# The values' products of layer 1 go two slots later in an order of instructions written by hand

## The chip, the cores and the metric

One core of a Trainium2 chip. The time is that of the whole kernel on the device, in microseconds (us), from one launch. TensorE is PE in the rows (PEld its weight loads), VectorE is DVE, ScalarE is ACT, GpSimd is POOL and SyncE, which issues most DMAs, is SP.

## The reference

Two transformer layers with a layer norm behind each half; batch 8, 512 tokens, width 256, all in float32.

```python
x = _layernorm(x + _L0_attn_ref(x, ...))   # 16 heads of 64, causal, latent of 64
x = _layernorm(x + _L0_ffn_ref(x, ...))    # 16 experts, the 2 best, and a shared one
x = _layernorm(x + _L1_attn_ref(x, ...))   # below
x = _layernorm(x + _L1_ffn_ref(x, ...))    # relu squared, 5 spiking steps
```

The change is in layer 1's attention. It has 16 heads of 16 columns per batch:

```python
q_c = jnp.einsum('bhtl,dl->bhtd', jnp.einsum('bhtd,ld->bhtl', xh, W_DQ), W_UQ)
q_c_norm = _rms_norm(q_c, q_norm_w)
q_r = jnp.einsum('bhtd,rd->bhtr', q_c_norm, W_QR)
kv = jnp.einsum('bhtl,dl->bhtd', jnp.einsum('bhtd,ld->bhtl', xh, W_DKV), W_UKV)
k_c, v_c = (kv[..., :HD], kv[..., HD:])
k_c_norm, k_r = _rms_norm(k_c, k_norm_w), jnp.einsum('bhtd,rd->bhtr', xh, W_KR)
scores = jnp.einsum('bhqd,bhkd->bhqk', q, k) * scale      # q = [q_c_norm, q_r], k = [k_c_norm, k_r]
ctx = jnp.einsum('bhqk,bhkd->bhqd', softmax(scores + causal), v_c)
out = jnp.einsum('bhtd,od->bhto', ctx, W_O)
```

The kernel multiplies the small matrices into four 128 x 128 ones beforehand (`w`: SQ for queries, SK for keys, SV for values with the output matrix in it, SG for the rotation part of the keys).

## The kernel before, in words

The kernel runs in blocks: layer 0's attention, its experts, and then one block for `layer1`. In that block every engine walks through the same list of slots, `SLOTS_ALL`, numbered from -52 to beyond 128, and issues in each slot what stands there. Nothing is scheduled by a tool: the order on each engine is the order of the code, and semaphores tie the engines together. Slots have no fixed length; a slot lasts as long as its work and its waits.

Slot n from 0 to 127 computes the scores of head n (`scores`, L1663, on TensorE, four tiles in the three banks `ps_score`) and VectorE takes the masked maximum of each tile (`mask_max`, L2037). Four heads make a quad. After a quad, TensorE turns its maxima (`turn_max`, L1673), ScalarE copies them (`keep_max`, L1874), and SyncE moves them by a DMA (`shifts`, L1474) into a row of the queries' buffer, so that the next product subtracts them. Seven slots behind (`BACK`), TensorE computes the same head's scores again, transposed and with the maximum taken off, in three groups (`exponents`, L1685): the first two behind the scores, the third at the very end of the slot, in two banks `ps_st` in turn. ScalarE takes the exponential of each group (`exps`, L1884), and GpSimd cuts off the triangle above the diagonal (`cut`, L1573). A quad's products with the values are in `attend` (L1701), in two slots per quad (remainder 0 and 1 of n by 4); `turn_back` (L1710) and VectorE's `outputs` (L2047 to L2054) finish them. `attend` waits until the `outputs` of the quad before are computed (L2049), since both use bank y.

What prepares queries, keys and values is the *front*. There is one per 8 heads, 16 in all. Each front f runs through steps, and `front_at(n, step)` tells which front has that step in slot n:

```python
def front_at(n, step):
    f, left = divmod(n + LEAD - step, HH)      # LEAD 23, HH 8
    return f if left == 0 and 0 <= f < NFRONT else None
```

So step s of front f stands in slot 8f + s - 23, and every step has a fixed remainder of the slot number by 8: step 12 has 5, steps 13 and 14 have 6 and 7, step 15 has 0. A turn of eight slots thus holds parts of three or four fronts. The steps are: -1 `turn` (L1607: x turned, into bank a), 0 `features` (ScalarE's copy of it, L1828), 1 and 2 `project` (L1619: queries, keys, bank b), 2 and 3 copies and squares (L1836, L1842), 3 and 4 `means` on VectorE (L2012), 5 to 8 GpSimd's root and `normed` (L1510 to L1530), 9 `turn_queries` (L1630, bank a), 10 the queries' high and low words (L1861, L1976), 11 `turn_keys` (L1640, bank b), 12 `weigh` on ScalarE (L1867) and on TensorE `values` (L1650, four products of 128 x 128 columns into bank a) and `rotation` (L1645, bank b), 13 `rotary` on VectorE (L2019) and `keep_values` on ScalarE (L1848: bank a into the values' buffer V), 14 the keys' high and low words (L1858, L1974). SyncE's `fill` (L1462, L1469, nine DMAs for a quad) then spreads the words into the buffers QS and KS.

Bank a is used in turn by `turn`, `turn_queries` and `values`. `turn` of front f waits for `keep_values` of front f - 2 (semaphore `vc`), and it stands in slot 8f - 24; `values` waits until the low words of the queries are out of bank a (`lo`). `attend` waits for `vc` too, 20 slots or more later. `keep_values` stands near the head of its slot on ScalarE, ahead of the slot's `exps`.

In every second turn (remainder by 16) there is more work: gathers of the experts' outputs on GpSimd, their mixing on VectorE (L1999), roots, and the norms' writes on ScalarE (L1890, L1896). Scores run from slot 0 on. Before it, fronts 0 and 1 run with TensorE mostly idle.

Of the kernel before, what the change touches and what calls it, by code (L numbers as in the profile page):

```python
# [1339 lines left out]
def layer1(nc, X, folded, slot, weight, Y, C, A):  # L1340

    with ExitStack() as ctx:
# [69 lines left out]
        def front_at(n, step):  # L1412

            f, left = divmod(n + LEAD - step, HH)
            return f if left == 0 and 0 <= f < NFRONT else None

        def turned(n):

            return (n - 5) // QUAD if 5 <= n < NHEADS + 5 and n % QUAD == 1 else None
# [31 lines left out]
        with nc.Block() as blk:  # L1451
# [147 lines left out]
            def _(pe):  # L1599
# [43 lines left out]
                def rotation(f):  # L1643
                    pe.wait_ge(s_kw, f + 1)
                    pe.matmul(ps_b[:], w[:, SG, :], xs[f % 2][:], start=True, stop=True).then_inc(s_g, 1)  # L1645

                def values(f):
                    pe.wait_ge(s_lo, 2 * f + 1)
                    for t in range(TT):
                        last = pe.matmul(ps_a[:, P * t:P * (t + 1)], xs[f % 2][:, P * t:P * (t + 1)],  # L1650
                                         w[:, SV, :], start=True, stop=True)
                    last.then_inc(s_v, 1)

                def scores(n):
                    u, j = n // QUAD, n % QUAD
                    if j == 0:
                        pe.wait_ge(s_rd[u % NQ], 9 * 16 * (u // NQ + 1))
                    for g, tiles in enumerate(SGROUP):
                        if n:
                            pe.wait_ge(s_max, (n - 1) * TT + tiles[-1] + 1)  # L1660
                        for i in tiles:
                            keys = P * (i + 1)
                            last = pe.matmul(ps_score[g][:, SCOL[i]:SCOL[i] + keys],  # L1663
                                             QS[u % NQ][:, j, P * i:P * (i + 1)], KS[u % NQ][:, j, 0:keys],
                                             start=True, stop=True)
                        last.then_inc(s_score, 1)
# [72 lines left out]
                for n in SLOTS_ALL:  # L1739
                    if n == 0:  # L1740
                        pe.wait_ge(s_share, 2 * NLATE)
                    if 0 <= n < NHEADS:
                        scores(n)
                    if turned(n) is not None:
                        turn_max(turned(n))
                    if BACK <= n < NHEADS + BACK:
                        exponents(n - BACK, (0, 1))
                    if n == TURN0:
                        pe.wait_ge(s_lo, 2 * NFRONT)
                        pe.wait_ge(s_vc, NFRONT)  # L1750
                        pe.wait_ge(s_x, TT)
                        FFN.turn(pe, 0)
                    if n == TURN1:
                        pe.wait_ge(s_x, 2 * TT)
                        FFN.turn(pe, 1)
                    if n == UP0:
                        pe.wait_ge(s_max, TT * NHEADS)
                    if UP0 <= n < UP0 + NF:
                        FFN.up(pe, 0, n - UP0)
                    if n >= 12 and n % QUAD == 0 and (n - 12) // QUAD < NQUADS:  # L1760
                        attend((n - 12) // QUAD, (0,))
                    if n >= 12 and n % QUAD == 1 and (n - 13) // QUAD < NQUADS:
                        attend((n - 13) // QUAD, (1, 2, 3))
                    if front_at(n, 12) is not None:
                        values(front_at(n, 12))
                        rotation(front_at(n, 12))
                    if front_at(n, 11) is not None:
                        turn_keys(front_at(n, 11))
                    if front_at(n, 9) is not None:
                        turn_queries(front_at(n, 9))  # L1770
                    if front_at(n, 1) is not None:
                        project(front_at(n, 1), 0)
                    if front_at(n, 2) is not None:
                        project(front_at(n, 2), 1)
                    if front_at(n, -1) is not None:
                        turn(front_at(n, -1))
                    if n >= 12 and n % QUAD == 2 and (n - 14) // QUAD < NQUADS:
                        turn_back((n - 14) // QUAD)
                    if n == LATE:
                        up(2)  # L1780
                    if n == LATE + 2:
                        up(3)
                        down(2)
                    if n == LATE + 6:
                        down(3)
                    if BACK <= n < NHEADS + BACK:
                        exponents(n - BACK, (2,))
# [15 lines left out]
            def _(act):  # L1803
# [40 lines left out]
                def keep_values(f):  # L1844
                    act.wait_ge(s_v, f + 1)
                    if f >= NV:
                        act.wait_ge(s_y, 2 * (f - NV) + 2)
                    act.activation(V[f % NV][:, :, :, 0:HD],  # L1848
                                   ps_a[:].rearrange("p (t h d) -> p t h d", t=TT, h=HH),
                                   ACT.Copy).then_inc(s_vc, 1)  # L1850
# [48 lines left out]
                for n in SLOTS_ALL:  # L1899
                    if n >= 12 and n % QUAD == 2 and (n - 14) // QUAD < NQUADS:  # L1900
                        u = (n - 14) // QUAD
                        act.wait_ge(s_y, u + 1)
                        if u >= 1:
                            act.wait_ge(s_yt, u)
                            act.wait_ge(s_sum, u)
                        act.activation(yq[:], ps_y[:], ACT.Copy).then_inc(s_yc, 1)
                    if front_at(n, 10) is not None:
                        high(front_at(n, 10), 0)
                    if front_at(n, 12) is not None:
                        weigh(front_at(n, 12))  # L1910
                    if front_at(n, 13) is not None:
                        keep_values(front_at(n, 13))
                    if front_at(n, 14) is not None:
                        high(front_at(n, 14), 1)
                    if front_at(n, 2) is not None:
                        keep(front_at(n, 2), 0)
                    if front_at(n, 3) is not None:
                        keep(front_at(n, 3), 1)
                    if front_at(n, 0) is not None:
                        features(front_at(n, 0))  # L1920
                    if turned(n) is not None:
                        keep_max(turned(n))
                    if BACK <= n < NHEADS + BACK:
                        exps(n - BACK, (0, 1))
                    if front_at(n, 2) is not None:
                        square(front_at(n, 2), 0)
                    if front_at(n, 3) is not None:
                        square(front_at(n, 3), 1)
                    if n == TURN0 + 1:
                        act.wait_ge(s_lo, 2 * NFRONT)  # L1930
                        FFN.keep(act, 0)
                    if n == UP0:
                        act.wait_ge(s_max, TT * NHEADS)
                        act.wait_ge(s_share, 2 * NLATE)
                    if n == UP0 + QUAD:
                        act.wait_ge(s_y, NQUADS - 1)
                    if UP0 <= n < UP0 + NF:
                        FFN.hide(act, 0, n - UP0)
                    if n == TURN1 + 1:
                        FFN.keep(act, 1)  # L1940
                    if n == UP1:
                        act.wait_ge(s_y, NQUADS)
                        for f in range(NF):
                            FFN.hide(act, 1, f)
                        FFN.keep(act, 2)
                    if n == LATE:
                        parts(2)
                    if n == LATE + 2:
                        parts(3)
                    for b, t in tiles_at(n, NORM):  # L1950
                        combined(b, t)
                    for b, t in tiles_at(n, WRITE):
                        write(b, t)
                    if BACK <= n < NHEADS + BACK:
                        exps(n - BACK, (2,))
# [220 lines left out]
```

## Time and profile before

| | |
|---|---|
| median of 3 runs | 1720.36 us (1720.34 to 1720.68) |
| profiled execution, its own time | 1719.73 us |
| its span, first to last instruction | 1717.9 us |
| TensorE busy in the span | 1588.0 us (92%) |
| VectorE / ScalarE / GpSimd busy | 1213.4 / 1014.5 / 468.3 us |
| mean granted TensorE clock | 0.973 |
| values' products | from 1028.5 us (front 0) to 1401.2 us (front 15) |
| slot 0 begins / slot 127 begins | 1047.91 us / 1449.55 us |

Times in the profile count from the first instruction. A slot is cut from the first score matmul of its head to the first of the next. In an idle entry, "[0.32 <-ACT c_probs L1884]" says that the engine stood idle for 0.32 us before this instruction and that ScalarE's instruction on line 1884 released it. In rows of the timeline the first number is the start and the second the time from there to the end of the merged instructions, so neighbouring matmuls overlap a little.

### The profile page before, as it was taken

Reading aid. Unit: us, or ns where it says so; the run is one execution under the profiler, and the core shown is the slowest. Engines: PE = TensorE matmul, PEld = TensorE weight load, DVE = VectorE, ACT = ScalarE, POOL = GpSimd, SP = SyncE. Lnnn points to the kernel's source line nnn. Section 1 sums busy time; section 2 is a strip of 40 time slices with the busy share of each in tenths; the row PEclk is TensorE's granted clock in tenths of the full one; section 3 lists DMA queues with packets and bytes.
Section 4 is the critical chain, followed back from the end, with each engine's and each line's share of the span. In section 5 each row is a group of like instructions: output and inputs, shape, how many; then the busy total and the mean of one; then the engine's idle time right before and its main releaser. Section 6 shows DMA issues by size and latency. Waiting matters only on the chain. (4 is left out here: it accounts for less than half of the span.)

```text
span 1717.9 us, 29270 instructions
## 1 busy us (share of the span) xinstructions
PE 1588.0 (92%) x9060; PEld 1102.0 (64%) x9060; DVE 1213.4 (71%) x4130; ACT 1014.5 (59%) x2544; POOL 468.3 (27%) x853
## 2 busy tenths in 40 slices
PE   7999999999999999968799876999999988899996
PEld 5667676767676767654688654666666655376765
DVE  5887878787878888836755466889988876134345
ACT  4876767676766667624444364767777766644340
POOL 4001000010101010100375376767775543100001
PEclk9999999999999999989899987999999999999998
DMA  5121111111111211102165528667766754000000
GB/s 164 41 53 38 38 41 48 36 44 50 44 44 44 50 39 40 40 4 95 38 178 164 114 69 123 91 97 112 103 99 90 92 76 100 1 6 25 13 25 31
DMA packets 72582, 111.67 MB, mean 65 GB/s; under 512 B 13264, under 2 KB 38320, under 8 KB 72304
## 3 DMA queue, kind: packets, MB, share of 16 engines
q1 hardware_dynamic: 61024, 81.04, 24.0%
q0 software_dynamic: 10016, 26.48, 6.9%
q10 hardware_dynamic: 1392, 2.29, 0.4%
q8 instruction: 76, 1.25, 0.3%
q14 instruction: 74, 0.61, 0.2%
HBM read 40.04 MB, written 18.87 MB: 34 GB/s over the span
## 5 line engine op out<-in xcount | busy, mean ns | idle before, releaser
L394 ACT ACTIVATE c_probs<-c_probs,a_negmax 128x128 f32<-128x128 f32 (+3 forms) x512 | 279.5, 550 | 0.0
L1884 ACT ACTIVATE c_probs<-a_ps_st 128x384 f32<-128x384 f32 (+1 forms) x384 | 191.9, 532 | 111.4 <-PE a_ps_st L1685 109.5
L2037 DVE CUSTOM_DVE_ANT_0 a_junk<-a_ps_score,c_mask 128x128 f32<-128x128 f32 (+3 forms) x512 | 220.2, 487 | 51.5 <-PE a_ps_score L1663 48.9
L399 ACT ACTIVATE c_probs<-a_ps_trans 128x512 f32<-128x512 f32 (+1 forms) x256 | 124.7, 487 | 214.1 <-PE a_ps_trans L300 213.2
L472 DVE CUSTOM_DVE_ANT_0 c_probs<-a_ps_score,c_mask 128x128 f32<-128x128 f32 (+3 forms) x512 | 219.6, 486 | 15.2 <-PE a_ps_score L281 14.1
L300 PE MATMUL a_ps_trans<-c_ident,c_probs 128*128 128x128 f32 x1280 | 187.9, 277 | 17.4 <-DVE c_probs L489 15.7
L300 PEld LDWEIGHTS a_ps_trans<-c_ident,c_probs 128*128 128x128 f32 x1280 | 146.5, 141 | 87.3 <-issue 39.3
L575 POOL TENSOR_SCALAR a_rstd<-a_mv 128x4 f32<-128x4 f32 x8 | 1.8, 229 | 689.6 <-DVE a_mv L502 689.6
L1685 PE MATMUL a_ps_st<-a_qs,a_ks 128*128 128x512 f32 (+3 forms) x512 | 151.2, 365 | 29.2 <-ACT c_probs L1884 21.8
L280 PE MATMUL a_ps_score<-a_kh,a_qs 128*128 128x128 f32 (+3 forms) x512 | 167.2, 350 | 1.7 <-issue 1.6
L489 DVE TENSOR_SCALAR c_probs<-c_probs,a_recip 128x128 f32<-128x128 f32 (+3 forms) x512 | 164.7, 386 | 4.5
L281 PE MATMUL a_ps_score<-a_kl,a_qs 128*128 128x128 f32 (+3 forms) x512 | 164.9, 322 | 0.0
L315 PE MATMUL a_ps_y<-c_probs,a_latv 128*64 128x512 f32 (+3 forms) x1024 | 151.9, 439 | 0.5 <-ACT c_probs L399 0.5
L1573 POOL TENSOR_SCALAR_AFFINE_SELECT c_probs<-c_probs 128x256 f32<-128x256 f32 x256 | 107.5, 429 | 142.2 <-ACT c_probs L1884 142.1
L1685 PEld LDWEIGHTS a_ps_st<-a_qs,a_ks 128*128 128x128 f32 x512 | 88.2, 192 | 86.6 <-ACT c_probs L1884 44.0
L464 DVE TENSOR_TENSOR a_qlow<-a_ps_q,a_qs 64x512 fp32r<-64x512 f32 x128 | 88.1, 688 | 71.8 <-ACT a_qs L388 69.3
L1663 PE MATMUL a_ps_score<-a_ks,a_qs 128*128 128x128 f32 (+3 forms) x512 | 117.0, 346 | 5.1 <-DVE a_negmax L2037 4.7
L261 PE MATMUL a_ps_q<-a_xT,a_wqk 128*128 128x512 f32 x256 | 120.5, 593 | 0.0
L315 PEld LDWEIGHTS a_ps_y<-c_probs,a_latv 128*64 128x64 f32 x1024 | 67.8, 136 | 80.0 <-issue 70.0
L1302 ACT ACTIVATE a_xs<-a_ps_score 128x512 f32<-128x512 f32 x64 | 38.2, 597 | 115.9 <-issue 82.4
L342 PE MATMUL a_ps_kv<-a_wvo,a_yT 128*128 128x256 f32 x464 | 105.1, 379 | 0.7 <-ACT a_yT L413 0.7
L280 PEld LDWEIGHTS a_ps_score<-a_kh,a_qs 128*128 128x128 f32 x512 | 97.0, 189 | 5.7 <-issue 3.2
(290 smaller groups left out, 3150.3 us busy)
## 6 DMA issues: line engine op xcount, KB each, us to landing
a_qs<-a_qlow SPq DMA_DIRECT2D x128, 128.0 KB, 2.2
slot_out<-m_y SPq DMA_DIRECT2D x80, 128.0 KB, 2.2
a_qs<-a_words_even SPq DMA_DIRECT2D x64, 128.0 KB, 4.3
a_ks<-a_words_even SPq DMA_DIRECT2D x64, 128.0 KB, 5.6
c_X<-in_x SPq DMA_DIRECT2D x8, 512.0 KB, 4.0
token_rows<-c_X SPq DMA_DIRECT2D x8, 512.0 KB, 5.7
a_qs<-a_counts SPq DMA_DIRECT2D x32, 128.0 KB
a_qs<-a_hid SPq DMA_DIRECT2D x32, 128.0 KB
```

The lines of the kernel that those rows point to most:

```text
L261: last = pe.matmul(ps_q[:], wqk[:, k, P * p:P * (p + 1)], xT[b % 2][:, k, :], start=k == 0, stop=k == KT - 1)
L280: pe.matmul(to, q, kh[b % 2][:, 0:keys], start=True, stop=False)
L281: last = pe.matmul(to, q, kl[b % 2][:, 0:keys], start=False, stop=True)
L300: last = pe.transpose(ps_trans[(3 * n + grp) % 2][:, col:col + P], prob[:, n % 4, QOFF[i] + P * k:QOFF[i] + P * (k + 1)], C.ident[:])
L315: last = pe.matmul(ps_y[LD * c:LD * (c + 1), P * k:L], latv[g // NPAIR % 2][:, k, :], probT[:, (2 * g + c) % 4, at:at + L - P * k], start= ...
L394: act.activation(at, at, ACT.Exp, scale=-1.0, bias=negmax[:, n % 4, i:i + 1], accum_out=rowsum[:, n % 4, i:i + 1]).then_inc(s_exp, 1)
L399: act.activation(probT[:, n % 4, TGCOL[grp]:TGCOL[grp] + TGLEN[grp]], ps_trans[(3 * n + grp) % 2][:, 0:TGLEN[grp]], ACT.Copy).then_inc(s_p ...
L472: dve.tensor_tensor_reduce(out=prob[:, n % 4, QOFF[i]:QOFF[i] + keys], in0=ps_score[grp][:, SCOL[i]:SCOL[i] + keys], in1=C.mask[:, L - key ...
L489: dve.tensor_scalar(at, at, recip[:, n % 4, i:i + 1], None, ALU.mult).then_inc(s_norm, 1)
L1685: last = pe.matmul(ps_st[item % 2][:, col:col + KLEN[c]], KS[u % NQ][:, j, P * c:P * (c + 1)], QS[u % NQ][:, j, P * c:L], start=True, stop ...
L1884: act.activation(probT[:, r8, col:col + width], ps_st[item % 2][:, 0:width], ACT.Exp).then_inc(s_stc, 1)
L2037: dve.tensor_tensor_reduce(out=junk[:, to:to + keys], in0=ps_score[g][:, at:at + keys], in1=C.mask[:, L - keys:L], scale=-1.0, scalar=3.0e ...
```

## The change

`values` leaves step 12 for step 14, on TensorE, so it goes from the slot with remainder 5 to the one with remainder 7, where it stands between the second and third group of exponents. `keep_values` goes from step 13 to step 15 on ScalarE, from remainder 6 to remainder 0. Each is issued in the same number, with the same waits and the same semaphores; `turn` of front f and `keep_values` of front f - 2 now stand in the same slot.

```diff
                     if front_at(n, 12) is not None:
-                        values(front_at(n, 12))
                         rotation(front_at(n, 12))
+                    if front_at(n, 14) is not None:
+                        values(front_at(n, 14))
                     if front_at(n, 11) is not None:
                         turn_keys(front_at(n, 11))
...
                     if front_at(n, 12) is not None:
                         weigh(front_at(n, 12))
-                    if front_at(n, 13) is not None:
-                        keep_values(front_at(n, 13))
+                    if front_at(n, 15) is not None:
+                        keep_values(front_at(n, 15))
                     if front_at(n, 14) is not None:
                         high(front_at(n, 14), 1)
```

## Rows read from the trace of the kernel before

**Rows 1.** page of the profiled execution, its first line
```profile
span 1717.9 us, 29270 instructions
```

**Rows 2.** windows: slots 45-48, 118, 37-52; us, PE PEld DVE ACT POOL busy, PEclk, DMA
```profile
1189.57:1194.87 5.30, 5.09 (x46) 3.21 (x45) 4.88 (x14) 2.78 (x6) 4.68 (x8) 1.00 1.10 136
1194.87:1197.36 2.49, 2.17 (x15) 1.54 (x14) 2.01 (x9) 2.30 (x5) 1.72 (x3) 1.00 0.43 114
1197.36:1199.46 2.10, 1.53 (x10) 1.11 (x10) 1.94 (x8) 1.95 (x6) 1.58 (x5) 1.00 0.04 12
1199.46:1202.61 3.15, 3.08 (x22) 1.70 (x22) 3.08 (x13) 1.90 (x5) 2.82 (x8) 1.00 0.98 160
1423.80:1425.86 2.06, 2.06 (x15) 1.54 (x14) 1.58 (x7) 1.86 (x4) 0.41 (x1) 1.00 0.78 92
1163.66:1215.59 51.93, 47.86 (x354) 32.05 (x354) 47.40 (x175) 38.07 (x83) 39.11 (x81) 1.00 0.73 104
```

**Rows 3.** waits, steady stretch 1072 to 1450: us in all, times, longest
```profile
PE a_ps_st L1685 <- ACT c_probs L1884: 15.6, 31, 1.7
...
PE a_ps_a L1630 <- POOL a_raw_q L1530: 1.3, 6, 0.3
```

**Rows 4.** timeline of PE, slots 45 to 48
```profile
1192.83 1.16 PE L1650 MATMUL a_ps_a<-c_w,a_xs 128*128 128x128 f32 x8
1193.83 1.02 PE L1645 MATMUL a_ps_b<-a_xs,c_w 128*128 128x512 f32 x2
...
1197.07 0.45 PE L1685 MATMUL a_ps_st<-a_qs,a_ks 128*128 128x256 f32 x2 [0.32 <-ACT c_probs L1884]
...
1199.18 0.44 PE L1685 MATMUL a_ps_st<-a_qs,a_ks 128*128 128x256 f32 x2 [0.57 <-ACT c_probs L1884]
...
1200.94 1.07 PE L1701 MATMUL a_ps_y<-c_probs,a_v 128*32 128x512 f32 x8
1201.94 0.66 PE L1607 MATMUL a_ps_a<-c_ident,c_X 128*128 128x128 f32 x4
```

**Rows 5.** the line of the values' products, whole kernel
```profile
L1650 PE MATMUL a_ps_a<-c_w,a_xs x128: 273/275/421, 1028.5 to 1401.2; 128*128 128x128 f32 x128
```

**Rows 6.** timeline of ACT, slots 46 to 48
```profile
1195.93 0.61 ACT L1848 ACTIVATE a_v<-a_ps_a 128x512 f32<-128x512 f32 x1
1196.40 1.00 ACT L1884 ACTIVATE c_probs<-a_ps_st 128x512 f32<-128x512 f32 x2
...
1198.53 0.98 ACT L1884 ACTIVATE c_probs<-a_ps_st 128x512 f32<-128x512 f32 x2
...
1200.59 0.98 ACT L1884 ACTIVATE c_probs<-a_ps_st 128x512 f32<-128x512 f32 x2 [0.21 <-PE a_ps_st L1685]
```

**Rows 7.** timeline of DVE, slots 46 and 47
```profile
1195.35 0.29 DVE L2037 CUSTOM_DVE_ANT_0 a_junk<-a_ps_score,c_mask 128x128 f32<-128x128 f32 x1 [0.80 <-PE a_ps_score L1663]
...
1200.38 0.42 DVE L2049 TENSOR_TENSOR a_yq<-a_ps_y,a_recip 128x256 f32<-128x256 f32 x1
```

**Rows 8.** L1474's landing times; one issue, its landing, its use (PE); L1469's landing times
```profile
DMA to landing us min/median/max: 1.8/5.0/6.5
...
1165.10 0.55 SPq L1474 DMA_DIRECT2D a_qs<-a_shift  x1
...
DMA to landing us min/median/max: 6.5/6.5/6.5
...
1172.13 0.72 PE L1685 MATMUL a_ps_st<-a_qs,a_ks 128*128 128x512 f32 x2
...
DMA to landing us min/median/max: 3.4/5.0/8.1
```

**Rows 9.** timeline of PE and ACT around the first scores
```profile
1045.51 1.91 PE L1650 MATMUL a_ps_a<-c_w,a_xs 128*128 128x128 f32 x8
...
1045.76 0.69 ACT L1867 ACTIVATE a_counts<-a_ps_b,c_qk_norm 128x512 f32<-128x512 f32 x1 [0.60 <-PE a_ps_b L1640]
...
1051.27 0.92 PE L1663 MATMUL a_ps_score<-a_ks,a_qs 128*128 128x128 f32 x3 [1.71 <-DVE a_negmax L2037]
```

## The prediction

> **What bounds the kernel now.** I began with the page, for the span of the profiled execution [rows 1], then cut the stage of layer 1's attention into single slots with the windows view. Sixteen slots, two turns of the front, take 51.93 us; in them TensorE is busy for 47.86 us and VectorE for 47.40, ScalarE for 38.07, at a granted clock of 1.00, the upper level of 2.4 GHz [rows 2]. So TensorE leads, VectorE is close behind, and 4.07 us in 16 slots, 2.0 per turn of eight, is all that a better order can win back from TensorE. The single slots say where that lies. The heaviest slot (remainder 5 of the slot number by 8, which I call slot 5) takes 5.30 us, TensorE 5.09 busy; slot 6 takes 2.49 with 2.17 busy; slot 7 takes 2.10 with 1.53 busy; slot 0 takes 3.15 with 3.08 busy [rows 2]. The waits view says what ended the idle time: most of it is `exponents` waiting for ScalarE's `exps` (15.6 us, 31 times) [rows 3]. In the timeline that is 0.32 us in slot 6 and 0.57 us in slot 7, in front of the third group of exponents each time [rows 4]. The reader should see that the values' products stand in the slot that has no idle time, and that two slots later TensorE stands still.
>
> **The change, part by part.** The values' products run 16 times, once per front; each time eight recorded matmuls, of 128 [rows 5]. They start at 1192.83 and the rotation behind them at 1193.83 [rows 4], so they take 1.00 us net. Fronts 3 to 15, thirteen of them, have slot 5 in the steady stretch; fronts 0 to 2 are told below.
>
> (a) *Slot 5 loses the products*: 1.00 us less. Nothing else in it ends later, since `rotation` needs only ScalarE's `weigh`, issued at the head of the slot. 5.30 becomes 4.30.
>
> (b) *Slot 6 loses the copy on ScalarE.* `keep_values` takes 0.61 us from 1195.93, and only then `exps` starts, at 1196.40 [rows 6]; TensorE's 0.32 us wait hangs on that. Without the copy the slot should look like slot 118, late in the stage, which has the same work on TensorE and no front: 2.06 us, all busy [rows 2]. 2.49 becomes 2.06, so 0.43 less.
>
> (c) *Slot 7 takes the products*, between its second and third group of exponents. The 0.57 us wait stands in exactly that place. The `exps` that it waits for starts at 1198.53 [rows 6] whatever TensorE does meanwhile, so 1.53 busy plus 1.00 gives 2.53 instead of 2.10: 0.43 more. The cover is complete: the products are longer than the wait.
>
> (d) *Slot 0 takes the copy* at its head on ScalarE. `exps` starts there at 1200.59 after 0.21 us of idle time [rows 6]; it will start up to 0.4 us later. TensorE needs it at the slot's third group, behind `attend` (1.07 us from 1200.94) and `turn` (0.66 us from 1201.94) [rows 4], more than 1 us after. And `turn`, which now waits for a copy in its own slot instead of one two slots back (both use bank a), comes a microsecond after that copy's end. Cost 0, hidden by `attend`; without that cover 0.6 per turn.
>
> (e) *VectorE* now has less time in slots 5 to 7. It waits 0.80 us for slot 6's scores [rows 7]; with them a microsecond earlier it is there about 0.2 late. That lag lasts until `outputs` of slot 7, whose product ends at 1200.80 (1200.38 and 0.42) [rows 7], while `attend` in slot 0, which needs it, starts at 1200.94 [rows 4]: no room. I charge 0.12 per turn there, between 0 (the lag dies out) and 0.40 (it is carried on through the next slots as well).
>
> (f) *GpSimd's chain* to the normed queries holds TensorE for 1.3 us in all, 6 times [rows 3]. Slot 7's longer time lies inside that chain, so most of this wait goes: 0.10 per turn.
>
> (g) *The shift transfer.* SyncE issues it in slot 5, and `exponents` of slot 7 needs it. An early one was issued at 1165.10, took 6.5 us to land, and was used at 1172.13 [rows 8]: 7.03 us of room. The change takes 1.43 us out of that (1.00 in slot 5 and 0.43 in slot 6) and leaves 5.60. All these transfers have a median of 5.0 and a longest of 6.5 us [rows 8], so some come late: 0.9 us for the longest. For the thirteen I take 1.8 us in all, two or three stalls of 0.3 to 0.9. The bounds are 0 (all land by the median) and 0.9 each, 11.7 us. The value is near the lower end because the median lies 0.6 under the room.
> The Trainium skill, DMA: Bandwidth & Descriptors (Anatomy of one DMA), gives about 2.0 us of fixed cost for a DMA from GpSimd plus its bytes, which for a small transfer would leave this one always early, and the sum 1.8 us lower. The trace speaks against it as a price here: 5.0 us at the median.
> No other queue changes its order. The fill of the query and key buffers behind the wait for slot 6's exponents starts 1.4 us earlier, with the same number of issues.
>
> (h) *The beginning.* In front 1, values start at 1045.51 and take 1.91 us, and the rotation stands behind them, though `weigh`, which it needs, is over at 1046.45 [rows 9]. Scores of slot 1 wait 1.71 us for VectorE's maximum [rows 9], and that hangs on the rotation through two words of the keys. Rotation 0.8 us earlier; I take 0.6, between 0 and 0.8. Front 0's rotation has no such delay and front 2's slots wait for VectorE anyway: 0.
>
> **Sum.** Per turn: -1.00 - 0.43 + 0.43 + 0.12 - 0.10 = -0.98. Thirteen turns: -12.7. Beginning: -0.6. Shift: +1.8. Together -11.5 us. The profiled execution took 1719.73 us (1.83 around its span), so 1708.2. The median of the runs, 1720.36, lies 0.63 above it; by the median it would be 1708.9. I take 1708.5, between the two, and count the rivals from 1720.0. A difference of 0.2%, 3.4 us, is about what a measurement of this kernel can tell from none.
>
> **Rivals.**
> *VectorE becomes the bound.* For it: 47.40 of 51.93 us busy already [rows 2], and with 2 us less per 16 slots it would be 95% busy. Against: its idle time before slots 6 and 7 is what the change uses, and the relation to TensorE in slots 1 to 5 stays. At the upper bound of (e), 0.40 per turn, the gain is 13 x 0.70 + 0.6 - 1.8 = 7.9, so 1712. Chance 0.20.
> *The copy and the products are hidden better than I say*: no shift late, no lag, slot 7 longer by 0.33 instead of 0.43, the queries' wait of (f) gone. 13 x (1.00 + 0.43 - 0.33 + 0.10) + 0.8 = 16.4, so 1703.6. Chance 0.14.
> *Nothing comes of it.* The time taken from slot 5 comes back as waits for the shift in slot 7: if each of the thirteen took the longest 6.5 us, 11.7 us go back and 1.6 are left, 1718.5. For it: the early one with 6.5. Against: the median. Chance 0.05.
> *Slower.* The same transfer, but worse: it now shares the DMA engines with the fill that starts at the head of slot 7, earlier than before. It decides from a mean landing of 5.60 + 1.02 = 6.6 us after its issue. The fill's own transfers take up to 8.1 us [rows 8]; at that price the stall is 2.5 us per turn, 32.5 in all, less 13.3 gained: 19 slower, 1739. Against: even the 6.5 us one had landed, at 1171.6, when slot 7's exponents asked for it at 1172.13. Chance 0.04.
> The Trainium skill, DMA: Bandwidth & Descriptors (Issuing engines are not separate DMA queues), says that DMAs of all issuing engines interleave on the same 16 DMA engines; that is this rival's mechanism, and its chance is the one just given.
>
> **How the numbers follow.** The forecast has 0.57, VectorE 0.20, the better case 0.14, nothing 0.05, slower 0.04. Faster by over 0.2% are the first three, 0.91; within 0.2% the fourth, 0.05; slower 0.04. The range takes in the forecast with its bounds, the VectorE case and most of the better one: 1703.5 to 1713.5.
>
> **What would show it.** In the profile after: slots 5, 6, 7 and 0 of one turn at 4.3, 2.1, 2.5 and 3.2 us; the values' products directly behind the second group of exponents of slot 7, and no wait for `exps` behind them; the wait for `exps` down from 15.6 to some 3 us; new waits of `exponents` for the DMA of the shift, 2 us in all; the wait for VectorE in front of `attend` in slot 0 up to 0.2 us; scores of slot 0 (the first) unchanged, those of slot 1 some 0.6 earlier. I am wrong if slot 6 keeps its 0.32 us wait, if scores in slots 6 to 1 wait for VectorE's maximum, or if the shift waits exceed 5 us together.

## The result, and the profile after

| | before | after |
|---|---|---|
| median, measured side by side | 1720.35 us (4 runs, 1719.07 to 1720.68) | 1703.31 us (4 runs, 1701.04 to 1705.65) |
| profiled execution, its own time | 1719.73 us | 1704.8 us |
| its span | 1717.9 us | 1702.8 us |

The ratio is 0.9905, with a 95% interval of 0.9894 to 0.9917. The change saves 17.0 us where I forecast 11.5. The median lies 0.2 us under the low end of my range and nearly on the "better hidden" rival (1703.6): the direction is right, the size short by a third.

The page of the kernel after, its first line, against [rows 1]:

```profile
span 1702.8 us, 29270 instructions
```

I cut slots in the same way as before. Windows of the kernel after; the columns are those of [rows 2]. In order: a slot 5, the slot 6 behind it, a slot 7 and the slot 0 behind it of a later turn (slots 79 and 80), then slots 108 and 120.

```profile
1187.58:1191.99 4.41, 4.19 (x38) 2.33 (x37) 4.30 (x14) 2.78 (x6) 3.80 (x8) 1.00 1.07 129
1191.99:1194.03 2.04, 2.04 (x14) 1.53 (x14) 2.04 (x8) 1.84 (x4) 1.74 (x2) 1.00 0.83 119
1293.67:1296.00 2.33, 2.33 (x19) 2.16 (x18) 2.33 (x12) 2.01 (x6) 1.73 (x6) 1.00 0.11 33
1296.00:1299.11 3.11, 3.07 (x23) 1.69 (x22) 3.04 (x13) 2.26 (x6) 2.86 (x7) 1.00 1.00 151
1381.79:1384.66 2.87, 2.87 (x23) 1.67 (x22) 2.80 (x11) 1.52 (x4) 2.27 (x5) 1.00 1.07 141
1416.18:1418.64 2.46, 2.46 (x18) 1.27 (x18) 1.88 (x9) 1.52 (x4) 1.10 (x3) 1.00 1.11 128
```

Slot 5 went from 5.30 to 4.41, slot 6 from 2.49 to 2.04, both nearly as forecast. Slot 7 takes 2.33 and not 2.53. The last two windows are the surprise, and they need the same two slots of the kernel before:

```profile
1392.88:1397.08 4.20, 4.20 (x23) 2.40 (x22) 2.30 (x9) 1.47 (x3) 2.80 (x7) 0.65 1.10 124
1429.69:1433.73 4.04, 4.04 (x18) 1.74 (x18) 2.25 (x10) 1.51 (x4) 1.22 (x3) 0.58 1.10 127
```

The same work took 4.20 instead of 2.87 and 4.04 instead of 2.46: in both, the granted clock of TensorE fell from the upper level (2.4 GHz, 1.00 in the column) to the lower (1.2 GHz) for most of the slot. In the kernel after it didn't.

The waits of the kernel after in the same part of the stage as [rows 3] (its slots are about 15 us earlier at the end); us in all, times, longest:

```profile
PE a_ps_st L1685 <- DMA a_qs<-a_shift: 3.1, 6, 1.2
PE a_ps_st L1685 <- ACT c_probs L1885: 2.3, 4, 0.6
ACT c_shared_gu L1859 <- DVE a_counts L2020: 1.5, 7, 0.4
PE a_ps_y L1701 <- DVE a_yq L2050: 1.4, 5, 0.4
PE a_ps_a L1630 <- POOL a_raw_q L1530: 0.5, 3, 0.2
```

The wait of `exponents` for `exps` falls from 15.6 us to 2.3. That for the shift rises from 2.4 us (2 times) to 3.1 (6 times). Of the small ones, that of `attend` for VectorE rises from 0.6 to 1.4, that of `turn_queries` for GpSimd falls from 1.3 to 0.5. New is a wait of ScalarE for `rotary` (L2020) in front of the keys' high word (L1859).

**Where the time went.** I compared all 128 slots of the two traces, and later those of a second pair on another chip (e5 and e7 below). The sums are over slots 8 to 111, thirteen turns, in us, after minus before:

| term of the forecast | forecast | first pair | second pair |
|---|---|---|---|
| slot 5: products gone (a) | -13.0 | -11.6 | -11.9 |
| slot 6: copy gone (b) | -5.6 | -5.7 | -5.3 |
| slot 7: products and shift waits (c, g) | +7.4 | +3.7 | +2.3 |
| slots 0 and 1: copy, VectorE's lag (d, e) | +1.6 | +1.4 | +0.6 |
| slot 2: the queries' chain (f) | -1.3 | -2.1 | -1.6 |
| slots 3 and 4, mostly of the last turn | 0 | -2.0 | +0.4 |
| slots 1 to 7 and 112 to 126 | 0 | -1.4 | -2.5 |
| start of slot 1 to start of slot 127 | -10.9 | -17.7 | -18.0 |
| everything ahead of slot 1 (h) | -0.6 | +2.6 | -2.7 |

Late shift transfers lengthen slots 39, 47 and 55 of the first pair, which took 3.09, 2.56 and 2.86 us where the others of their kind take 2.33: 1.5 us of its 3.7. (Of the 3.1 us of idle time that the waits view puts down to the shift only 0.8 lie in these thirteen turns, in slots 39 and 55, and in slot 47 only the weight load waits. The rest is in slots 7, 107, 115 and 119.) The other 2.2 are 0.17 a turn. In the second pair only slot 39 stands out, 2.69 against 2.32, so by 0.4.

Two terms account for the difference: slot 7 grew by much less than forecast, and TensorE's clock fell less often late in the stage. The last row differs in sign between the pairs. In the first, 2.1 of the 2.6 us were there already at the first `turn_queries` (1022.1 before, 1024.2 after), ahead of anything that the change moves. So it is the spread of single executions, and the medians of several runs hold less of it.

Now one turn in detail. TensorE in slots 79 and 80 after, to be read against [rows 4]:

```profile
1293.67 0.85 PE L1663 MATMUL a_ps_score<-a_ks,a_qs 128*128 128x128 f32 x4
1294.37 0.57 PE L1685 MATMUL a_ps_st<-a_qs,a_ks 128*128 128x512 f32 x2
1294.77 1.05 PE L1650 MATMUL a_ps_a<-c_w,a_xs 128*128 128x128 f32 x8
1295.71 0.45 PE L1685 MATMUL a_ps_st<-a_qs,a_ks 128*128 128x256 f32 x2
1296.00 0.85 PE L1663 MATMUL a_ps_score<-a_ks,a_qs 128*128 128x128 f32 x4
...
1298.44 0.66 PE L1607 MATMUL a_ps_a<-c_ident,c_X 128*128 128x128 f32 x4
1298.85 0.36 PE L1685 MATMUL a_ps_st<-a_qs,a_ks 128*128 128x256 f32 x1
```

The products stand behind the second group of exponents and nothing waits behind them; slot 0's third group, at 1298.85, doesn't either, so the copy (d) is covered. The other two engines in the same turn, ScalarE first, against [rows 6] and [rows 7]:

```profile
1294.54 0.63 ACT L1859 ACTIVATE c_shared_gu<-a_counts 128x512 fp32r<-128x512 f32 x1 [0.17 <-DVE a_counts L2020]
1295.07 0.96 ACT L1885 ACTIVATE c_probs<-a_ps_st 128x512 f32<-128x512 f32 x2
...
1296.79 0.60 ACT L1849 ACTIVATE a_v<-a_ps_a 128x512 f32<-128x512 f32 x1
1297.26 0.99 ACT L1885 ACTIVATE c_probs<-a_ps_st 128x512 f32<-128x512 f32 x2
```

```profile
1293.13 0.69 DVE L2038 CUSTOM_DVE_ANT_0 a_junk<-a_ps_score,c_mask 128x512 f32<-128x512 f32 x1
1293.74 0.08 DVE L2038 DVE_READ_ACCUMULATOR2_ANT a_negmax<- 128x1 f32 x1
1293.74 0.68 DVE L2020 TENSOR_TENSOR a_counts<-a_counts,a_ps_b 128x512 f32<-128x512 f32 x1
```

Here is what slot 7 runs into. VectorE takes slot 6's last maximum, then `rotary` (1293.74, 0.07 behind the slot's start; in the kernel before it started 0.36 ahead of it). ScalarE's high word of the keys waits 0.17 for that, and `exps`, queued behind it, starts 1.40 after the slot's start instead of 1.17 to 1.28. TensorE's third group needs `exps`. This is a chain through VectorE and ScalarE that holds the slot at 2.3 us, with or without the products in it (e1, e8). The forecast charged the slot's length to the products.

Five of the thirteen turns look different. There a write (L1891) stands ahead of the last `exps` of slot 6, and the high word begins behind that `exps`, without a wait for `rotary`, at nearly the same distance from the slot's start. ScalarE in slot 71 (from 1268.94), and TensorE:

```profile
1268.87 0.60 ACT L1891 ACTIVATE c_X<-c_X,a_cbias,a_crstd 128x256 f32<-128x256 f32 x1
1269.36 0.49 ACT L1885 ACTIVATE c_probs<-a_ps_st 128x384 f32<-128x384 f32 x1
1269.81 0.63 ACT L1859 ACTIVATE a_words_even<-a_counts 128x512 fp32r<-128x512 f32 x1
```

```profile
1269.62 0.72 PE L1685 MATMUL a_ps_st<-a_qs,a_ks 128*128 128x512 f32 x2
1270.18 1.05 PE L1650 MATMUL a_ps_a<-c_w,a_xs 128*128 128x128 f32 x8
```

The products start 0.56 behind the exponents in front of them and not 0.40, since the bank of the second group is freed by that `exps`. By starts TensorE's own order then fills 2.3 us as well. These slots took 2.25 before and the others 2.11, so slot 7 grew by about 0.1 in the five turns and by about 0.2 in the eight, where the shift isn't late.

The beginning (h) gained nothing. Front 1's rotation after, PE again:

```profile
1048.91 2.07 PE L1645 MATMUL a_ps_b<-a_xs,c_w 128*128 128x512 f32 x2 [0.78 <-ACT a_counts L1868]
```

It took 1.25 us before and 2.07 now, since it runs at the lower clock level (granted 0.63 from 1030.0 to 1052.3, and 0.50 from 1048.9 to 1050.2; before, 0.89 from 1047.4 to 1048.7). From the end of `weigh` to the start of `rotary` it is 2.13 us before and 2.24 after. The products in front of it had cost nothing.

### The profile page after: what moved, and what is told of

The parts are those of the page before. It is cut to its first block and busy times, and to the rows that moved or that the text cites. A ratio compares the mean times of both kernels' runs of the same rounds, so it can differ in the third digit from the quotient of the medians.

```text
span 1702.8 us, 29270 instructions
## 1 busy us (share of the span) xinstructions
PE 1584.4 (93%) x9060; PEld 1102.6 (65%) x9060; DVE 1213.1 (71%) x4130; ACT 1016.8 (60%) x2544; POOL 470.8 (28%) x853
## 3 DMA queue, kind: packets, MB, share of 16 engines
q8 instruction: 76, 1.25, 0.3%
```

## Experiments

Kernels of one group ran on one chip beside the kernel before, and ratios are against those runs. No kernel below leaves out work; e6 adds transposes whose result nobody reads.

### First group: which part brings what (kernel before beside it: 1717.23 us, 11 runs)

**e1: the copy alone moves.**

```diff
-                    if front_at(n, 13) is not None:
-                        keep_values(front_at(n, 13))
+                    if front_at(n, 15) is not None:
+                        keep_values(front_at(n, 15))
```

> The products stay in slot 5; only their copy on ScalarE goes from slot 6 to slot 0. My theory: the 0.32 us wait of slot 6 hangs on the copy, so slot 6 is 2.06 instead of 2.49 in thirteen turns, slot 5 stays 5.30 and slot 7 keeps its 0.57 us wait: 5.7 us faster than before, about 1714.6. Rival: the place of the products brings everything and the copy only follows: no change, 1720. A second rival: the copy at slot 0's head delays exps there by up to 0.4 us and TensorE feels it: the gain of slot 6 given back in slot 0.

Measured: 1714.64 us (1711.64 to 1717.1), ratio 0.9981 (0.9970 to 0.9992), so 2.6 us faster. Slots 6, 7 and 0 of one turn:

```profile
1270.69:1272.75 2.06, 2.06 (x14) 1.53 (x14) 1.58 (x7) 1.86 (x5) 0.41 (x1) 1.00 0.48 128
1272.75:1275.06 2.31, 1.69 (x10) 1.12 (x10) 2.31 (x10) 2.31 (x7) 1.57 (x5) 1.00 0.12 36
1275.06:1278.20 3.14, 3.08 (x22) 1.70 (x22) 3.00 (x13) 2.28 (x6) 2.81 (x8) 1.00 1.01 153
```

Slot 6 gains its 0.44 a turn with the copy alone: (b) is right. But slot 7 takes 2.31 with no products in it, and waits 0.62 us of that for `exps`. So the products aren't needed for that length. I had expected 5.7 us and measured 2.6. By the traces, over slots 8 to 111, slot 6 gives 5.7, and slot 7 takes back 2.0, slots 0 and 1 take back 2.5. That is in part the second rival, but not by its mechanism: nothing in slot 0 waits for `exps`; in slot 80 `attend` waits 0.21 us for VectorE.

**e2: the products go to slot 6, the copy to slot 0.**

```diff
-                        values(front_at(n, 12))
                         rotation(front_at(n, 12))
+                    if front_at(n, 13) is not None:
+                        values(front_at(n, 13))
```

> Products in slot 6 (step 13) instead of slot 7, the copy in slot 0 as in the changed kernel. My theory: what counts is that slot 7 has a wait to fill. Slot 5 loses 0.89, slot 6 loses the copy's 0.44 and gains 0.8 to 0.9 of products, slot 7 keeps its 0.57 us wait: about 0.5 per turn, 6 to 7 us faster than before, 1713 to 1714. Rival: it is the balance alone, any slot lighter than slot 5 does as well: 1703, as the changed kernel.

Measured: 1707.26 us (1705.58 to 1708.4), ratio 0.9943 (0.9927 to 0.9960), so 10.0 us faster. Slots 6 and 7:

```profile
1265.83:1268.44 2.61, 2.61 (x23) 2.52 (x22) 2.61 (x10) 2.39 (x5) 1.08 (x3) 1.00 0.62 129
1268.44:1270.55 2.11, 1.54 (x10) 1.11 (x10) 1.84 (x8) 1.92 (x5) 1.19 (x4) 1.00 0.07 17
```

Slot 6 grows by 0.55 over e1's 2.06 and not by the products' 1.00, since part of them lies in room that was there; slot 7 keeps its 2.11 and its idle time. The two slots take 4.72 together, against 4.37 (2.04 and 2.33) with the change: slot 7 is the better place by 0.35 a turn. I had expected 6 to 7 us; slot 6 takes 2.61 against 2.49 before, 0.12 more and not the 0.4 of my sum.

**e3: fronts 0 and 1 as before, the others as after.**

```diff
+                    if front_at(n, 12) is not None and front_at(n, 12) < 2:
+                        values(front_at(n, 12))
                     if front_at(n, 12) is not None:
                         rotation(front_at(n, 12))
-                    if front_at(n, 14) is not None:
+                    if front_at(n, 14) is not None and front_at(n, 14) >= 2:
...
+                    if front_at(n, 13) is not None and front_at(n, 13) < 2:
+                        keep_values(front_at(n, 13))
```

> The changed kernel, but fronts 0 and 1, which run before the scores, keep products and copy where they were. By my prediction these fronts give 0.6 us of the gain, so this is 0.6 slower than the changed kernel. Rival, from the two traces: the rotation that comes earlier runs at the lower level of the clock (2.07 us instead of 1.25) and eats the gain, so the difference is between 0 and 0.5 us the other way.

Measured: 1702.31 us (1701.02 to 1706.46), ratio 0.9920 (0.9904 to 0.9937). The interval overlaps that of the change (0.9894 to 0.9917), and a few tenths of a us can't be told in it. It doesn't support my 0.6 us of (h), and it can't rule it out either.

**e4: as after, but ScalarE issues the shift transfer itself behind its copy.**

```diff
                     act.activation(shift[u % 2][:], ps_st[item % 2][0:QUAD * TT, 0:P], ACT.Copy).then_inc(s_stc, 1)
+                    act.wait_ge(s_stc, item + 1)
+                    act.dma_start(QS[u % NQ][ONE:ONE + 1, :, :]..., shift[u % 2][:]...).then_inc(s_shift, 16)
...
-                    if turned(n) is not None:
-                        shifts(turned(n))
```

> The changed kernel, but ScalarE issues the shift's DMA itself, right behind its copy, instead of SyncE behind the nine transfers of a fill. Theory A: the 5 us to landing are the queue of SyncE's transfers ahead of it; then it lands in 2 to 3 us, all waits for the shift (3.1 us in the changed kernel's profile) are gone and it is 3 us faster than the changed kernel, about 1700. Theory B: the DMA engines are shared, so it lands after 5 us as before, and ScalarE loses 0.55 us per issue in slots 5 and 1: same as the changed kernel or up to 3 us slower.

Measured: 1704.55 us (1702.04 to 1705.46), ratio 0.9920 (0.9904 to 0.9937). Landing times of the shift transfer, whole kernel, of the kernel after and then of e4:

```profile
DMA to landing us min/median/max: 1.8/5.1/7.3
```

```profile
DMA to landing us min/median/max: 1.8/5.1/7.6
```

It lands no sooner from another engine's queue: the waits are 3.5 us in 5 times against 3.1 in 6. The 5 us are not time behind other issues on SyncE. In the same kernel the transfer with which a fill begins (L1462), also of 8 KB, lands after 1.9 us at the median, so the size isn't the cause either. That fits the transfer sharing the DMA engines with the fill's, which the Trainium skill, DMA: Bandwidth & Descriptors (Issuing engines are not separate DMA queues), gives as a rule; the trace doesn't show the sharing itself.

### Second group: the clock, and a second pair (kernel before beside it: 1728.96 us, 21 runs)

This chip takes longer for the same kernel: the span of e5 is 9.1 us longer than that of the first profile (1727.0 against 1717.9), and 7.4 us of that lie ahead of slot 1 (1058.65 against 1051.27). Another 3.9 lie in slot 5, which takes 5.57 to 5.92 in nine of the thirteen turns; in the changed kernel (e7) it is 4.64 to 5.03 in the same nine. Why stays open. The difference of the pair is 0.91 a turn for slot 5, as on the first chip.

**e5: the kernel before, unchanged**, profiled once more.

> The kernel before once more, with a profile of its own, beside the next two. In the first profile the granted clock falls to the lower level in slots 108 and 120, each behind a slot in which TensorE waits 0.94 or 1.45 us for the shift and 0.57 us for exps. Theory A (the clock fell because of these waits, and does so in every run): both falls are there again, at 1.3 and 1.6 us. Theory B (chance of one run): they are elsewhere or missing. The time itself: 1717 to 1720 either way.

**e6: the kernel before, with transposes put in front of the wait for the shift**, 7 in slot 107 and 11 in slot 119.

```diff
                     if j == 0 and 0 in rs:
+                        for _ in range({107: 7, 119: 11}.get(m + BACK, 0)):
+                            pe.wait_ge(s_rawc, 2 * NFRONT)
+                            pe.transpose(ps_b[:, 0:P], C.ident[:], C.ident[:])
                         pe.wait_ge(s_shift, 16 * (u + 1))
```

> The kernel before with idle time filled: 7 transposes of the identity into bank b in slot 107 and 11 in slot 119, in front of the wait for the shift; their results are not used. They take about as long as the waits they stand in. Theory A (idle time makes the clock fall): no fall in slots 108 and 120, which are 2.86 and 2.46 us as in the changed kernel: 2.9 us faster than before, with more work. Theory B: the clock falls there anyway, or the transposes cost what they take: same as before or up to 0.5 us slower.

Measured: e5 1729.19 us (1726.68 to 1732.5), ratio 1.0004 (0.9995 to 1.0013); e6 1728.26 us (1725.28 to 1731.04), ratio 0.9997 (0.9988 to 1.0006). Slots 119 and 120, e5 first, then e6:

```profile
1435.47:1439.60 4.13, 2.35 (x11) 1.35 (x10) 2.99 (x13) 1.51 (x4) 0.91 (x3) 0.79 0.46 96
1439.60:1444.11 4.51, 4.51 (x18) 2.21 (x18) 2.25 (x10) 1.47 (x3) 1.13 (x3) 0.50 1.08 125
```

```profile
1435.85:1439.58 3.73, 3.01 (x21) 2.30 (x21) 3.00 (x13) 1.47 (x4) 0.82 (x2) 1.00 0.39 94
1439.58:1442.06 2.48, 2.48 (x19) 1.28 (x18) 1.90 (x9) 1.52 (x4) 1.13 (x3) 1.00 1.10 126
```

In e5 slot 119 stands idle for 1.8 us (1.36 for the shift, 0.43 for `exps`), and slot 120 runs at 0.50. With the idle time filled for the most part, the clock stays up and slot 120 takes 2.48 instead of 4.51, so the fall costs 2.0 us there. That fits the theory that TensorE's idle time ahead brings the fall, but one execution doesn't show it, since the fall is missing in others with as much idle time (see e7). In slot 107 this execution of the kernel before had no wait for the shift and no fall (of my two falls only one came again), so that the seven transposes cost 1.1 us and gave 0.3 back in slot 108. In all e6's profile gains 0.6 us from slot 1 on. Its time, where I had expected 2.9 us less, is the same.

**e7: the changed kernel again.**

> The changed kernel once more, on the same chip as the others, with a profile of its own. Theory A (17 us is 13 turns at 1.05 and 3 us of clock that was lost in the kernel before): slots 5 and 6 again 0.89 and 0.44 shorter in all thirteen turns; the gain is 14 us where before has no falls of the clock and 17 where it has two. Theory B: all of the 17 us is in the turns: 17 us on this chip too, with thirteen turns at 1.3.

Measured: 1711.88 us (1708.18 to 1714.15), ratio 0.9904 (0.9889 to 0.9919): 17.1 us again. No fall of the clock late in the stage, though slot 119 stands idle for 1.97 us (1.40 and 0.57), more than in e5 on the same chip:

```profile
1417.51:1421.30 3.79, 1.82 (x10) 1.06 (x10) 3.00 (x13) 1.48 (x4) 0.81 (x2) 1.00 0.38 92
1421.30:1423.77 2.47, 2.47 (x18) 1.28 (x18) 1.89 (x9) 1.51 (x4) 1.11 (x3) 1.00 1.12 129
```

So the same slot with about the same idle time is followed by a fall in one execution and by none in another. Over all thirteen profiles slot 119 stood idle for 1.5 to 2.3 us in twelve; slot 120 then fell to 0.50 to 0.61 in nine of them (before, e1, e2, e4, e5, e8 to e11) and stayed at 1.00 in three (after, e3, e7), and also in e6 with 0.7 us idle. Slot 107 was idle for 1.5 us both before and in e2, and slot 108 fell only in the first.

**e8: the first of the four products in slot 6, the others in slot 7.**

```diff
-                    if front_at(n, 14) is not None:
-                        values(front_at(n, 14))
+                    if front_at(n, 13) is not None:
+                        values(front_at(n, 13), (0,))
+                    if front_at(n, 14) is not None:
+                        values(front_at(n, 14), (1, 2, 3))
```

> The changed kernel with the products split: tile 0 in slot 6 ahead of turn_back, tiles 1 to 3 in slot 7. In the run with products in slot 6 that slot grew by only 0.55 us for 0.8 us of products, so 0.25 us of it fell into a wait of turn_back; and slot 7 grew by 0.2 to 0.3 in the changed kernel. Theory A: the quarter is hidden in slot 6 and slot 7 has 0.2 less: 0.2 per turn, 2.6 us faster than the changed kernel. Theory B: VectorE, 95% busy, and the shift now bind there (slot 7 waits for what it gets earlier): less than 1 us faster, with more wait for the maxima and the shift.

Measured: 1713.52 us (1711.67 to 1716.27), ratio 0.9909 (0.9894 to 0.9923), the same as the change and not 2.6 us faster, as my theory A had it. Slots 6 and 7:

```profile
1323.92:1325.99 2.07, 2.07 (x17) 1.88 (x16) 1.59 (x7) 1.87 (x5) 0.41 (x1) 1.00 0.00 0
1325.99:1328.30 2.31, 2.31 (x16) 1.85 (x16) 2.31 (x12) 2.31 (x7) 1.58 (x5) 1.00 0.11 34
```

A quarter of the products is hidden in slot 6 at no cost, and slot 7 stays at 2.31 all the same. With none (e1), three quarters (e8) and all of the products it has one length.

### Third group: take the chain away (kernel before beside it: 1729.53 us, 12 runs)

In these the keys' high word goes behind the first of the two `exps` of its slot on ScalarE, so that `exps` no longer stands behind it. e9 has this on top of the change, e10 on top of e8, e11 on top of e1.

```diff
-                    if front_at(n, 14) is not None:
-                        high(front_at(n, 14), 1)
...
                     if BACK <= n < NHEADS + BACK:
-                        exps(n - BACK, (0, 1))
+                        exps(n - BACK, (0,))
+                    if front_at(n, 14) is not None:
+                        high(front_at(n, 14), 1)
+                    if BACK <= n < NHEADS + BACK:
+                        exps(n - BACK, (1,))
```

> The changed kernel, but ScalarE makes the keys' high word (step 14) behind the first of the slot's exps instead of ahead of both. Theory A (slot 7's length is set by the chain of VectorE's rotary, high word, exps, third group of exponents, and the products behind that chain are hidden): the chain is 0.2 us shorter, but the products end at the same point, so slot 7 stays 2.3: no change, within 1 us of the changed kernel. Theory B (the late high word alone is what made slot 7 longer than 2.11): slot 7 back to 2.11 to 2.2, 2 us faster.

> The same move of the high word on the kernel with split products (tile 0 in slot 6, tiles 1 to 3 in slot 7). Theory A: now neither the chain nor the products hold slot 7: it goes from 2.32 to about 2.12, 0.2 in thirteen turns, 2.6 us faster than the changed kernel. Theory B (something else holds it, VectorE's maximum for the scores): slot 7 stays at 2.3.

> The same move of the high word on the kernel in which only the copy moved, with no products in slot 7. Theory A: slot 7, 2.32 there, goes back to 2.11, the length of a slot with TensorE waiting for its own exponents only: 0.2 in thirteen turns, 2.6 us faster than with the copy alone, some 5.5 faster than before. Theory B: the copy itself, at slot 0's head, holds the turn; slot 7 stays 2.32.

Measured: e9 1714.40 us (1712.41 to 1716.73), ratio 0.9907 (0.9887 to 0.9928); e10 1715.34 us (1714.62 to 1717.77), 0.9921 (0.9900 to 0.9942); e11 1724.44 us (1721.48 to 1727.27), 0.9965 (0.9952 to 0.9979). Slot 7 of e10, then of e11:

```profile
1328.53:1330.63 2.10, 2.10 (x16) 1.78 (x16) 2.10 (x10) 1.84 (x5) 1.40 (x4) 1.00 0.04 12
```

```profile
1337.16:1339.27 2.11, 1.70 (x11) 1.13 (x10) 2.11 (x10) 1.85 (x5) 1.40 (x4) 1.00 0.04 12
```

Without the high word ahead of `exps` slot 7 takes 2.1 again, with three quarters of the products or with none. That shows the part of the chain on ScalarE; its beginning on VectorE (maximum, `rotary`) is read from the traces and wasn't moved. In e9, with all the products, the slot takes 2.17 in eight turns and 2.31 in the five with the write, between my two theories: in those five TensorE's own order is as long as the chain was. TensorE in a 2.17 one, and in the slot 0 behind it:

```profile
1353.30 0.85 PE L1663 MATMUL a_ps_score<-a_ks,a_qs 128*128 128x128 f32 x4
1353.99 0.57 PE L1685 MATMUL a_ps_st<-a_qs,a_ks 128*128 128x512 f32 x2
1354.40 1.05 PE L1650 MATMUL a_ps_a<-c_w,a_xs 128*128 128x128 f32 x8
1355.21 0.42 PE L1685 MATMUL a_ps_st<-a_qs,a_ks 128*128 128x256 f32 x2
1355.47 0.85 PE L1663 MATMUL a_ps_score<-a_ks,a_qs 128*128 128x128 f32 x4
...
1356.90 0.44 PE L1685 MATMUL a_ps_st<-a_qs,a_ks 128*128 128x384 f32 x1 [0.35 <-ACT c_probs L1885]
```

From start to start the products take 0.81 here. And in e9 and e10 nothing is won in the time (I had expected 2.6 us from e10), for the delay of ScalarE moves on: slot 0 now waits 0.35 for `exps`, and against the kernel before it grows by 0.3 a turn in e9 and by 0.4 in e10 and e11. e11 is 5.1 us under its kernel before, about the 5.5 expected, where e1 was 2.6 under; but the two intervals overlap, and by the traces slot 0 takes back more than slot 7 gives. None of the versions tried clearly beats the change.

## Why the prediction was right in kind and short in size

- **(a) Slot 5: right, 0.89 a turn and not 1.00.** The rotation takes 0.1 longer where it now stands, 1.13 behind `attend` against 1.02 behind the products. That is probably a gap of TensorE's own issue at the head of the weight load behind `attend`; the waits view has it for the products before and, with the same 2.6 us in 13 times, for the rotation after. It wasn't the products' to take along.
- **(b) Slot 6: exact**, 0.44 against 0.43, and by e1 the copy alone does it.
- **(c) Slot 7: the term that was mis-sized, the largest error.** The step was "so 1.53 busy plus 1.00 gives 2.53 instead of 2.10: 0.43 more". Measured +0.17 a turn (+0.06 to +0.26 in turns without a shift wait, both pairs). Two things were wrong in it. The 1.53 of busy time counts the modelled ends of matmuls that overlap the next; by starts the slot's own work is 1.36 (0.69, 0.41 and 0.26 in the rows of e9), and with 0.81 for the products 2.17, 0.07 more than 2.10. And the 2.10 was read from one slot: five of the thirteen slots 7 before take 2.25. What holds the slot instead is the chain maximum, `rotary`, high word, `exps` in eight turns (e1, e8, e10, e11); in the five with the write that chain and TensorE's own order are equally long. The sentence that `exps` comes at the same time "whatever TensorE does meanwhile" was wrong too: it comes 0.1 to 0.2 later.
- **(d) The copy in slot 0: right**, covered. In e2, which has it and slot 7 as before, slot 0 grows by 0.1 us in thirteen turns.
- **(e) VectorE's lag: real, but felt first elsewhere.** `attend` waits 0.8 us more for it in all, and slots 0 and 1 grow by 1.4 us in the first pair and 0.6 in the second, against 1.6. But its first effect is in slot 7, through `rotary`. The rival "VectorE becomes the bound" names this lag; at 0.40 a turn it was far too dear.
- **(f) The queries' chain: the size is right, the reason isn't shown.** The wait falls from 1.3 us to 0.5, and slot 2 gains 2.1 and 1.6. But it gains 1.8 in e1 and 1.2 in e2 as well, and e2 has no longer slot 7.
- **(g) The shift: right.** It lands as before (5.1 against 5.0 us) and comes late in three of the thirteen turns of the first pair, 1.5 us by the slots' lengths against 1.8; in the second pair in one, 0.4. The rivals "nothing" and "slower" needed landings near 6.6 as a rule, and fall. The median of 5.0 was that of all 32 transfers, though; the thirteen that slot 7 needs had a median of 5.3 before and 5.4 after, so the room over it was thinner than the 0.6 of the forecast, and that the 1.8 fitted is in part luck.
- **(h) The beginning: failed.** What I took for a queue on TensorE was time at the lower clock level; with the products away the rotation runs slowly by itself.
- **The signs of being wrong** named in the prediction didn't come, but for one small one: the wait in slot 6 is gone, the shift waits are 3.1 us together and not 5, and from slot 12 to slot 112 the scores wait for VectorE's maximum for 0.06 us in slot 39 and 0.17 in slot 105 only.
- **Not foreseen at all: the clock late in the stage.** By slots 108 and 120 it is 2.9 us in the first pair, by slots 120 and 121 some 2.3 in the second. e6 fits idle time of TensorE in front as the cause, but the same idle time is followed by no fall in e7 and in slot 107 of e2. e1, e2, e4 and e8 to e11 each had one such fall, e4 and e9 with the products where the change puts them. So part of this gain may come and go between executions; what decides it stays open, and it wasn't shown that it belongs to the change.
- **The rival "better hidden" has the number and not the mechanism.** Its 1703.6 is 0.3 from the median. But it wanted no late shift, no lag of VectorE and 0.33 for slot 7. The shift and the lag came, slot 7 grew by half of that, and 2 to 3 us of the traces' gain are the clock, which it doesn't have. That it meets the time is luck.

Slot 7 came out 3.7 us better than forecast in the first pair and 5.1 in the second, 3.4 and 3.6 of it by (c) and the rest by (g); the clock adds 2.9 and 2.3; (a) takes back 1.4 and 1.1. That makes 5.2 and 6.3 us, about the difference between 11.5 and 17.

## What to carry to other kernels

Work moved into a slot that waits is cheap, and its price is not the sum of busy times but what the slot is held by: measure its length by the starts of its instructions, and ask which chain through the other engines would hold it with the moved work taken out altogether. When one slot is shortened, look whether an engine that ran late in it hands the delay to a third one in the next. And lay the granted clock beside the slots before blaming their work: two slots out of 128 held a sixth of the difference between the first two traces, and it wasn't shown that the change brought it.

## What the runs showed of the hardware

- A fall to the lower clock level in slots 108 and 120 came behind a slot in which TensorE stood idle for 1.5 to 2.3 us, and cost 1.3 to 2.0 us (4.20 against 2.87, 4.51 against 2.48). It isn't certain: of twelve executions with such a slot 119, nine had the fall and three didn't, one of them with 1.97 us idle (e7).
- The shift transfer, 8 KB, lands after 5.1 us at the median, from 1.8 to 7.3, and the same when another engine issues it (e4). The 8 KB transfer at the head of a fill lands after 1.9.
- Eight matmuls whose merged row lasts 1.05 us held TensorE for 0.81 from their start to the start of the next work (e9).
- Executions differ by 1.7 to 2.7 us ahead of slot 1, in either direction, also where their kernels are alike up to there (e5 and e6, 1.7), and the chips by 12 us (medians of 1717.23 to 1729.53 for the kernel before). Only runs beside each other show a change of this size.
